# A fused attention and mixture-of-experts kernel: zeroing, row planes, scatters and banks regrouped, and eleven weight steps transposed once

## The reference

```python
x = x + attn(_layernorm(x))      # Wq, Wk, Wv: 512 -> 2048 (32 heads of 64)
#   q = relu(x Wq), k = relu(x Wk), v = x Wv
#   kv = k^T v per head;  out = (q kv) / clip(q . sum(k), 1e-6);  out @ Wo + bo
x = x + ffn(_layernorm(x))       # 8 experts, each token goes to its best 2
#   scores = x gate_w^T + gate_b + bias;  gates = softmax(top 2 scores)
#   h = silu(x w1[e]^T + b1[e])      (352 wide)
#   y = h w2[e]^T + b2[e];  out = sum over its 2 experts of gate * y
```

## Time and profile before

| | |
|---|---|
| time, median of 3 runs | 1029.01 us (1028.38 to 1030.11) |
| time of the profiled execution | 1029.53 us |
| its span, first to last instruction | 1027.8 us |
| TensorE busy | 995.1 us, 97% of the span |
| VectorE, ScalarE, GpSimd busy | 736.7, 543.3, 266.3 us |
| mean granted TensorE clock | 0.99 |

### The profile page before, as it was taken

The page is one execution under the profiler, slowest core; times in us unless marked ns, Lnnn a source line. Parts: engine busy times, 40 slices in busy tenths (PEclk is TensorE's granted clock), DMA queues, the critical chain, the costliest instruction groups (busy, mean ns, idle before and its releaser), DMA issues. The chain is left out here.

```text
span 1027.8 us, 17481 instructions
## 1 busy us (share of the span) xinstructions
PE 995.1 (97%) x4863; PEld 827.6 (81%) x4864; DVE 736.7 (72%) x1593; ACT 543.3 (53%) x1361; POOL 266.3 (26%) x423
## 2 busy tenths in 40 slices
PE   9998799999999999999899999999999979999998
PEld 7876688888888888888788887888888868888886
DVE  7876565565556567857788888888888866666665
ACT  4542544444444455865455555555555775555553
POOL 1000000000000002222644444444444752333334
PEclk9999899999999999999999999999999989999999
DMA  9999592000010011332211111111115854776873
GB/s 320 374 348 340 183 374 90 21 20 20 20 40 23 20 62 62 103 119 96 90 63 52 51 51 51 53 59 51 59 43 141 234 162 78 118 106 106 117 111 53
DMA packets 120254, 115.20 MB, mean 112 GB/s; under 512 B 47033, under 2 KB 94570, under 8 KB 120082
## 3 DMA queue, kind: packets, MB, share of 16 engines
q1 hardware_dynamic: 110962, 97.73, 31.3%
q0 software_dynamic: 9248, 16.95, 8.7%
HBM read 42.91 MB, written 63.35 MB: 103 GB/s over the span
## 5 line engine op out<-in xcount | busy, mean ns | idle before, releaser
L1013 ACT ACTIVATE qs<-q,nrec 128x64 f32<-128x64 f32 x512 | 129.6, 335 | 106.9 <-DVE nrec L1404 104.2
L621 POOL TENSOR_TENSOR wv_lo<-wv_in,wv_hi 128x512 fp32r<-128x512 f32 x4 | 5.2, 1292 | 417.3 <-ACT wo_hi L934 417.3
L1686 PE MATMUL pK<-wk_hi,xnT_hi 128*128 128x512 f32 (+1 forms) x256 | 101.0, 394 | 11.9 <-DVE xnT_lo L1259 11.8
L1686 PE MATMUL pA<-k_hi,xn_hi 128*128 128x512 f32 x256 | 101.0, 394 | 0.5 <-DVE k_lo L1279 0.5
L1686 PE MATMUL pK<-wq_hi,xnT_hi 128*128 128x512 f32 x256 | 100.5, 393 | 0.0
L1687 PE MATMUL pK<-wk_lo,xnT_hi 128*128 128x512 f32 (+1 forms) x256 | 100.4, 392 | 0.0
L1688 PE MATMUL pK<-wk_hi,xnT_lo 128*128 128x512 f32 (+1 forms) x256 | 100.2, 391 | 0.0
L1688 PE MATMUL pK<-wq_hi,xnT_lo 128*128 128x512 f32 x256 | 99.8, 390 | 0.0
L1688 PE MATMUL pA<-k_hi,xn_lo 128*128 128x512 f32 x256 | 99.8, 390 | 0.0
L1687 PE MATMUL pA<-k_lo,xn_hi 128*128 128x512 f32 x256 | 99.7, 389 | 0.0
L1687 PE MATMUL pK<-wq_lo,xnT_hi 128*128 128x512 f32 x256 | 99.7, 389 | 0.0
(11 more groups left out here) (281 smaller groups left out, 2503.0 us busy)
## 6 DMA issues: line engine op xcount, KB each, us to landing
xr_dram<-zero SPq DMA_DIRECT2D x8, 4352.0 KB, 28.8
w_in<-in_ffn_w SPq DMA_DIRECT2D x22, 256.0 KB, 3.2
w_in<-in_ffn_w SPq DMA_DIRECT2D x8, 704.0 KB, 6.1
xn<-in_attn_hidden_states SPq DMA_DIRECT2D x16, 256.0 KB, 6.4
wv_in<-in_attn_Wv SPq DMA_DIRECT2D x16, 256.0 KB, 2.7
wo_in<-in_attn_Wo SPq DMA_DIRECT2D x16, 256.0 KB, 2.9
wk_in<-in_attn_Wq SPq DMA_DIRECT2D x4, 1024.0 KB, 5.7
xnT_dram<-xnT SPq DMA_DIRECT2D x4, 1024.0 KB, 11.7
```

Of the source, the lines that this page charges most:

```text
L621: pool.tensor_tensor(wv_lo[:, b], wv_in[:, b], f(wv_hi[:, b]), ALU.subtract).then_inc(wv_lo_ready, 1)
L1013: i = nc.scalar.activation(qs[:, s], q[:, s], ACT.Copy, scale=nrec[:, b * HC + h:b * HC + h + 1])
L1686: nc.tensor.matmul(dst, lhs[0], rhs[0], start=start, stop=False)
```

## The change

1. Zeroing: the table is filled by ten equal DMAs of 14 row tiles (`ZROWS`), one in each of the ten turns of the Wv/Wo loop, after that turn's loads. None stands between the loads of the key weights.
2. Planes: ACT makes `xp` (for tile 14 `xp_last`), DVE that of tile 15; POOL makes none. `dots` alternates between two `gprod` tiles and waits only for the dot before the last.
3. Scatters: the last two tiles' rows go out in `put_slots`, right when their slots are known; their meta data go after `meta_row` (`rows_ready`), and the gather of `meta_in` after `put_b2(7)`. `load_tile` waits for `rows_ready` and no longer for `experts_ready`; `meta_transpose` moves behind h(0). The loads of w2 for experts 6 and 7 no longer wait for the gather.
4. The eleven steps: `subtract_hi` is the one matmul onto the bank that already holds the transposed blocks.
5. Experts: `gx`, `gT_hi`, `gT_lo` and the banks of h and y exist twice, so rows are merged two tiles ahead; `xgT` exists once. Load i now waits for the merge of tile i-1 instead of i-2. ACT's order per tile is h(i), merge and round (i+2), silu(i). The first merge moves ahead of the last two weight steps.

```diff
-            sp.wait_ge(zero_early, 1)
-            zero_rows(0, 3)
-            sp.wait_ge(wk_lo_ready, 2 * FB)
-            load_wk(2)
-            zero_rows(3, 6)
...
+            for c in range(1, NC):
+                sp.wait_ge(wk_lo_ready, c * FB)
+                load_wk(c)
...
                     load_pair(2 * h + b, b)
+                    sp.dma_start(xr_dram[ds((2 * h + (b - 2)) * (ZROWS * P), ZROWS * P), :].rearrange("(p r) (h n) -> p (r h) n", p=P, h=2),
+                                 zero16[:, :].unsqueeze(1).to_broadcast([P, 2 * ZROWS, D])).then_inc(xr_zeroed, 16)
...
             def load_tile(i):
-                if i >= 2:
-                    sp.wait_ge(rec_lo, i - 1)
-                    sp.wait_ge(rec_hi, i - 1)
+                if i >= 1:
+                    sp.wait_ge(rec_lo, i)
+                    sp.wait_ge(rec_hi, i)
...
+                put_rows(r, b)
                 if not isinstance(r, int) or r < NT - 2:
-                    put_rows(r, b)
-                for c in range(2):
-                    pool.indirect_dma_start(meta_dram, ...)
+                    put_meta(b)
...
+            def put_planes(t):
+                act.wait_ge(xn2_ready, t + 1)
+                if isinstance(t, int) and t == NT - 2:
+                    act.wait_ge(dots_done, E * t)
+                elif not (isinstance(t, int) and t == 0):
+                    act.wait_ge(s_xr, 32 * t)
+                to = xp_last if isinstance(t, int) and t == NT - 2 else xp
+                nc.scalar.copy(planes(to), words(xn2[:, :])).then_inc(xp_ready, 1)
...
+            def act_expert(i, b):
+                act_h(i, b)
+                if not isinstance(i, int) or i + 2 < NS:
+                    act_rec(i + 2, b)
+                    act_gT(i + 2, b)
+                act_silu(i)
...
             def subtract_hi(k):
                 pe.wait_ge(w_hi_ready, k + 1)
-                raw(k, False)
                 dst, rows, hi = w_step(k, w1_hi, w2_hi, w_bank(k))
-                nc.tensor.matmul(dst, neg_ident[0:rows, 0:rows], hi, start=False, stop=True).then_inc(w_sub_put, 1)
+                nc.tensor.matmul(dst, neg_ident[0:rows, 0:rows], hi, start=False, stop=True,
+                                 skip_group_check=True).then_inc(w_sub_put, 1)
...
+            pe_h(0, 0, expert(0))
+            meta_transpose()
+            pe_h(1, 1, expert(1))
```

More of the change, by code:

```diff
@@ L360, in block_kernel @@
         hT_ones = sem("hT_ones")
-        s_xt = [sem(f"s_xt{i}") for i in range(2)]
+        s_xt = sem("s_xt")
+        rows_ready = sem("rows_ready")
         rec_lo = sem("rec_lo")
@@ L694, in put_rows @@
             def put_rows(r, b):
-                rows = xp_last if isinstance(r, int) and r == NT - 1 else xp
+                rows = xp_last if isinstance(r, int) and r == NT - 2 else xp
                 pool.wait_ge(xp_ready, r + 1)
@@ L821, in _ @@
             put_b2(7)
+            pool.wait_ge(rows_ready, 1)
+            for b in range(2):
+                pool.wait_ge(s_meta[b], 16 * NT)
+            pool.indirect_dma_start(meta_in[:, :], None, meta_rows, bass.IndirectOffsetOnAxis(meta_row[:, :].bitcast(U32), 0)
+                                    ).then_inc(s_metain, 16)
             pool.wait_ge(experts_ready, 1)
@@ L1164, in _ @@
             w_act_lo(3)
-            for k in range(6, WSTEPS - 2):
+            for k in range(6, 43):
                 w_hi(k)
@@ L1195, in act_silu @@
                     act.wait_ge(hT_lo_ready, i)
-                for b in range(HB):
-                    w = min(P, H - b * P)
-                    last = nc.scalar.activation(hT[0:w, b * P:(b + 1) * P], pX[0:w, b * P:(b + 1) * P], ACT.Silu,
-                                                bias=b1T[0:w, ds(b * E + e, 1)])
+                for n in range(HB):
+                    w = min(P, H - n * P)
+                    last = nc.scalar.activation(hT[0:w, n * P:(n + 1) * P], pX[0:w, n * P:(n + 1) * P], ACT.Silu,
+                                                bias=b1T[0:w, ds(n * E + e, 1)])
@@ L1223, in _ @@
                 for b in range(2):
-                    act_tile_e(2 * h + b, b)
-            act_tile_e(NS - 1, 0, last=True)
+                    act_expert(2 * h + b, b)
+            for i in range(NS - 3, NS):
+                act_expert(i, i % 2)
         @block.vector
@@ L1954, in raw @@
                     i = nc.tensor.matmul(bank[0:w, b * P:(b + 1) * P], src, ident[:, :],
-                                         is_transpose=True, start=b == 0, stop=whole and b == FB - 1)
+                                         is_transpose=True, start=b == 0, stop=b == FB - 1)
                 return i
@@ L2034, in pe_hT @@
                 pe.wait_ge(h_ready, i + 1)
-                if not (isinstance(i, int) and i < 1):
+                if isinstance(i, int) and i == 0:
+                    pe.wait_ge(far_ready, 1)
+                else:
                     pe.wait_ge(hT_ready, i)
```

269 lines of the change are left out of this document (126 added, 143 removed).

## The result

The change makes the kernel slightly slower. Over 20 runs each, the kernel after takes 1031.27 us (median, 1028.83 to 1034.32) and the kernel before 1028.92 us (1026.78 to 1032.83). The ratio is 1.0022, with a 95% interval of 1.0013 to 1.0031. The profiled execution after took 1031.75 us with a span of 1029.9.

The account below looks back on a forecast made before the run. TensorE, busy 97% of the span, was taken as the bound, with gains where it waits. The terms -13.5 - 1.0 - 3.4 + 10.2 = -7.7 took the median from 1029.0 to 1021.3 us, range 1010 to 1033.

Parts of the forecast that it names:

- the term of the sum for the experts: Expert stage: row-load turns of 4.8 us against a tile of 4.49 cost +10.2 us over 33 tiles.
- the ring: Expert row loads: load i+1 waits for the merge of tile i; a turn is merge to issue, load, merge.
- The 0.72: Expert stage: time from merge to the next load's issue, 0.72 us, taken as a fixed part of the turn.
- the two bounds: Expert turn: 4.3 us without contention from scatter-adds, 5.3 us with it.
- the rival "hidden": Expert loads slip between the adds, turns of 4.3 us, tiles stay at 4.49: 1011.1 us, chance 18%.
- The slow ring: Every expert load meets an add, turns stay at 5.3 us: +26.4, in all 1037.5 us, chance 20%.
- The zeroing: Key stage: the gap ahead of chunk 1, the half pace and an earlier window's wait go: -13.5 us.
- Planes and dots: Query stage: steady tiles at 0 (-1 to +2), second `rank` -1.0 us.
- The eleven steps and the weights: Weight stage to h(2): earlier step 40 -1.9, earlier first merge -1.0, h(0) to h(2) -0.5; sum -3.4 us.
- The gate of step 40: End of the weight stage: step 40 follows the bias copies, which end earlier with one indexed DMA fewer: -1.9 us.
- the signs for right: TensorE not idle near 98 to 110, clock 1.00 there, step 40 some 16 us earlier, row loads 4.7 to 4.9 us apart.
- the signs for wrong: Row loads 4.49 apart with TensorE full, merges waiting with distance over 5.0, or TensorE waiting on pair weights during zeroing.

Follow-up runs that it names:

- experiment 4: Kernel after with each scatter-add of the expert stage replaced by a DMA of 64 bytes: 1012.81 us, a turn of 4.74 us.
- Experiments 4 to 6: Kernel after without the scatter-adds (1012.81 us), with the row number read ahead of the wait (1021.70 us), and with both edits (1001.25 us).
- experiment 7: Kernel after with the copy of planes back on POOL (1035.70 us), and kernel after with a single gprod buffer (1030.94 us).
- zeroing-only kernel: Kernel before with the moved zeroing DMAs alone: 1014.86 us, ratio 0.9865.
- both comparisons: Kernel after with the eleven steps transposed twice again: 1032.77 us; kernel before with zeroing and planes, without and with the steps transposed once: 1013.38 and 1013.24 us.
- experiment 1: Kernel before with one wait changed, so load i+1 waits for the merge of tile i, as with one row buffer: 1056.75 us.
- experiment 2: Kernel after with two row buffers and a single y buffer, y(i) waiting until scatter-add i-1 has landed: 1079.40 us.

## Why the prediction was wrong

**The step that failed** is the term of the sum for the experts: "I take the middle, 4.8 us, for the 33 tiles after the first adds: 33 x (4.8 - 4.49) = +10.2". The mechanism was right (the merges wait for their load in every tile, and the ring sets the pace), the size was not. A turn is 5.19 us, 0.39 over the forecast, and from h(2) to h(38) it costs 24.3 us and not 10.2. That alone turned a gain into a loss. Against 0.72 + 3.3 + 0.78 the measured turn has three differences:

- The merge starts 0.49 us after the last byte. The prediction read issue to last byte from DMA windows and left this out: +0.49.
- Merge to issue is 1.04 us and not 0.72. The 0.72 was one instance, of a kernel in which SP's read takes 0.27 us; in the ring its mean is 0.61 (experiment 4): +0.32.
- The last byte comes at 2.88 us, near the quiet load of 2.6 to 2.8 us and not in the middle of 2.8 and 3.8: -0.42.

The argument that the ring settles between the two bounds looked for contention in the load alone. Experiments 4 to 6 show that it moves: taken out of SP's read, it turns up in the load. Even without adds the turn is 4.74 us, so the rival "hidden", with 18%, had no chance here. The slow ring, with 20%, was what happened, with turns of 5.19 and not 5.3 us. Its argument against, "a longer period leaves more room between them", was true of the load and not of the turn.

The Trainium skill, page DMA: Bandwidth & Descriptors, section "Issuing engines are not separate DMA queues", has DMAs of all issuing engines interleave on the same 16 DMA engines. The runs agree: with the load issued early, issue to merge is 4.08 us among adds and 3.42 without them.

**The zeroing** (-13.5): right, -13.4 by its own run and -14.2 in the trace after. The ten new DMAs cost nothing that is seen. (They move 3584 KB each, in the unit in which the old ones move 4352, and not 3670.)

**Planes and dots** (-1.0): wrong in size. "TensorE is full in either case, and I cost the steady tiles at 0" was false: in the kernel before TensorE was busy 198.05 of the 200 us from 500 to 700 with 926 matmuls, and after 200.00 with 957. The bound of -1 us for the steady tiles was too narrow: they gained some 4 to 5 of the query stage's 6.8 us, and either edit alone is enough (experiment 7). At the second `rank` 0.7 us were won (a wait of 2.52 us gives way to one of 1.85 ahead of ACT's `qs`). I had looked for waits on TensorE and found one of 2.52 us; the loss was many small ones, which show in the distance from tile to tile.

**The eleven steps and the weights** (-3.4): near up to h(0), -2.8 in the trace where the prediction had -2.9. Its -0.5 from h(0) to h(2) was wrong in sign: that stretch became 1.7 us longer, at a granted clock of 0.69, which had been 0.81. The gate of step 40 did what was worked out: from `meta_row` to the last bias columns is 11.3 us in the zeroing-only kernel (808.44 to 819.76) and 9.3 us in the kernel after (803.07 to 812.37), -2.0 where -1.9 was predicted. That the transposes themselves are worth 0 held in both comparisons.

Of the signs for right, TensorE is not idle near 98 to 110, at a granted clock of 1.00. Step 40 starts 23.8 us before its old place (836.54 to 812.71) and not 16, and the loads are 5.19 us apart and not 4.7 to 4.9. One of the signs for wrong came, "the merges wait for a load in every tile and the distance is over 5.0".

## What to carry to other kernels

A buffer taken away closes a ring: price its whole turn (signal, read of the address, issue, last byte, from last byte to the consumer's start, consumer) by means over many instances under that stage's traffic, and test it by adding the one wait to the old kernel, as in experiment 1. A TensorE that is 99% busy is not full: take the distance from tile to tile and compare. And an edit whose sum is nothing may hold a part of 23 us that can be kept, so take its parts one by one.

## What the runs showed of the hardware

- SP's read of one number from SBUF takes 264 to 478 ns, with a median of 275, without scatter-adds, and in the ring beside them 266 to 1059 ns with a median of 477. The slow ones begin some 2 to 2.8 us after the start of an add's issue (experiment 4).
- The merge starts 0.49 us after the last byte of its load, in the mean of 34 turns of the kernel after.
- A scatter-add of 256 KB takes 4.90 us from issue to landing in the chain of experiment 2 and 4.8 in the median in the kernel after, against the 2.5 us that I had supposed.
- The Trainium skill, page SBUF — State Buffer, section "SBUF: two separate sides", says that a VectorE instruction with two SBUF inputs and a GpSimd one that reads SBUF take their shared port pair for the whole instruction, and the other waits. The group of dots that fall beside POOL's copy agrees: 14 dots of 1416 ns in the mean with the copy on POOL (the first row, planes on POOL) and of 700 ns with it on ACT (the second, the kernel after).

```profile
L1438 DVE SCALAR_TENSOR_TENSOR gprod<-xn,gw_late 128x512 f32<-128x512 f32 x14 | 19.8, 1416 | 0.0
```

```profile
L1438 DVE SCALAR_TENSOR_TENSOR gprod<-xn,gw_late 128x512 f32<-128x512 f32 x14 | 9.8, 700 | 0.0
```
